# A transformer layer over 16 pairs of sequences: the loop over the middle pairs written out as straight code

## The chip, the cores and the metric

One Trainium2 chip, one of its cores. The metric is the device time of one execution in microseconds (us), as the median of several runs. The profile comes from one execution taken by the hardware profiler.

## The reference

The input `x` has 32 sequences of 256 tokens with 128 features. One layer of attention with eight heads and no scaling, then a feed-forward part, each followed by a residual sum and a layer norm without weights:

```python
Q = (x @ Wq.T).reshape(b, n, H, R)          # H = 8, R = 64
K = (x @ Wk.T).reshape(b, n, H, R)
V = (x @ Wv.T).reshape(b, n, H, d)          # d = 128
attn = softmax(einsum('bnhr,bmhr->bhnm', Q, K))
x = layernorm(x + einsum('bhnm,bmhd->bnd', attn, V))
h = silu(tlin(x, w1_w, w1_s)) * tlin(x, w2_w, w2_s)     # 512 wide
h = gelu(tlin(h, h1_w, h1_s)); h = gelu(tlin(h, h2_w, h2_s))
x = layernorm(x + tlin(h, w3_w, w3_s))
```

`tlin(x, w, s)` is `(x @ w.T) * s`. The matrices `w*_w` and `h*_w` hold whole numbers from a set of three.

## The kernel before

The 32 sequences are worked on as 16 pairs (`PAIRS = 16`) of 512 tokens. Every matrix product is made exact enough for float32 by splitting each operand into a high part and a low part in a narrower format (`t_hi` and `t_lo`, `pt_hi` and `pt_lo`, and so on) and adding two or three products (lines 778, 779 and 780 in `three`, lines 859 to 862 in `layer`). ScalarE (ACT) mostly makes the high parts, VectorE (DVE) and GpSimd (POOL) the low parts.

The work is a software pipeline written by hand. Step `i` has 16 slots, one for each of the 16 attention units of a pair (8 heads times 2 sequences). In a slot TensorE (PE) makes the scores of a unit three slots ahead, turns the probabilities of the present unit, and multiplies those of two slots ago by V. Beside this, step `i` carries the feed-forward part of pair `i - 1`: the turned x1 in slot 4, layer 1 in slots 5 to 8, layer 2 in slot 9 together with the V products of the next pair, layer 3 in slot 12 together with the T products of the next pair, layer 4 in slot 14 and, in slot 15, the turning back of its result (`turns(YT_BANK, ... yt ...)`, line 785, which the profile names `bank<-ident,turns_buf`). Step `i` also carries the last norm and the store of pair `i - 2`. There are thus 18 steps, 0 to 17, and the flags of a step (`cur`, `nxt`, `ffn`, `tail`) say which of these parts it has.

Each engine runs its own program: the helper `steps` is called once for each of SP, POOL, ACT, DVE and PE with that engine's `step`. The engines are held together by counting semaphores alone. Steps 0 and 1 are straight code. Steps 2 to 11 are a loop of five iterations with two steps in each, since some buffers alternate between even and odd pairs (`xt_of`). Steps 12 to 17 are straight code again. In the loop the number of the pair is a register: `count` builds the value that a semaphore must reach out of it, in straight code the value is a constant.

In every feed-forward layer PE looks at a flag that it has loaded from the weights, and takes one of two versions of the layer's code: with the products of the weights' low parts (`emit(True)`, line 862 runs too) or without them (`emit(False)`). This `either` is met seven times in a step: four times in layer 1, once in each of layers 2, 3 and 4.

Of the kernel before, what the change touches and what calls it, by code (L numbers as in the profile page):

```python
# [75 lines left out]
def layer_kernel(nc, x, wq, wk, wv, w1_w, w1_s, w2_w, w2_s, h1_w, h1_s, h2_w, h2_s, w3_w, w3_s, out):  # L76
# [3 lines left out]
    PAIRS = B // 2  # L80
# [18 lines left out]
    with ExitStack() as ctx:  # L99
# [113 lines left out]

        def steps(eng, step):

            step((None, 0), True, True, False, False)
            step((None, 1), True, True, True, False)

            last = (PAIRS - 3) // 2 * 2
            with eng.Fori(2, last - 1, 2) as r:  # L220
                step((r, 0), True, True, True, True)
                step((r, 1), True, True, True, True)
            for i in range(last, PAIRS + 2):
                step((None, i), i < PAIRS, i + 1 < PAIRS, i <= PAIRS, True)

        G_ATT = 4
        PREP = [(a_hi[:, 0:4, :], a_lo[:, 0:4, :]), (a_hi[:, 4:8, :], a_lo[:, 4:8, :]),
# [71 lines left out]
        def _(sp):  # L301
# [18 lines left out]
            def step(i, cur, nxt, ffn, tail):  # L320
# [6 lines left out]
                if exists(plus(i, 3)):  # L327
                    sp.wait_ge(s_xt_mm, count(i, 1, 3))
                    sp.dma_start(x_in[:, :, :], x_rows[row(plus(i, 3))]).then_inc(s_xin, 16)

            steps(sp, step)
            sp.wait_ge(s_yfree, 16 * PAIRS)

        @block.gpsimd
        def _(pool):
# [38 lines left out]
            def step(i, cur, nxt, ffn, tail):  # L374
                f, g = plus(i, -1), plus(i, -2)
                for j in range(J):
# [22 lines left out]
                    for c in range(KC):  # L399
                        if j == L2_SLOT and not tail:  # L400
                            lo_part(f, c, even_hi, even_lo, s_2hi, s_2lo)
                        if j == L3_SLOT and not alone(f):
                            lo_part(f, c, odd_hi, odd_lo, s_3hi, s_3lo)

            steps(pool, step)

        @block.scalar
        def _(act):
# [78 lines left out]
            def step(i, cur, nxt, ffn, tail):  # L487
                f, i1, i2 = plus(i, -1), plus(i, 1), plus(i, 2)
                for j in range(J):
# [56 lines left out]
                    if ffn and j == L4_SLOT:  # L546
                        act.wait_ge(s_l4, count(f, 1, 1))
                        if cur:
                            act.wait_ge(s_at, count(i, 2, 1))
                        nc.scalar.activation(yt[:, :], L4_BANK[:, :], ACT.Copy,  # L550
                                             scale=scales[:, 4 * KC:4 * KC + 1]).then_inc(s_yt, 1)

            steps(act, step)

        @block.vector
# [541 lines left out]
```

## Time and profile before

| | |
|---|---|
| median of 3 runs | 1096.17 us (1095.11 to 1096.27) |
| span of the profiled execution, first to last instruction | 1095.1 us |
| mean granted clock of TensorE over the span | 0.987 |
| PE busy | 1051.1 us, 96% |
| DVE busy | 819.5 us, 75% |
| ACT busy | 811.4 us, 74% |
| POOL busy | 602.9 us, 55% |

The time of the profiled execution outside its span is not recorded. The median lies 1.07 us above the span. In the views, a row with PE is a matmul, PEld its weight load, and a row with a q behind the engine's name is an instruction of that engine's sequencer, such as a branch or a sum in a register; these do not count as busy time.

### The profile page before, as it was taken

How to read it: one execution, taken by the hardware profiler on the slowest of the kernel's cores; microseconds unless marked ns; L12 is line 12 of the kernel's file. 1: busy time of each engine (PE TensorE's matmuls, PEld its weight loads, DVE VectorE, ACT ScalarE, POOL GpSimd, SP SyncE). 2: the span in 40 equal slices, each digit the busy share in tenths (PEclk: the TensorE clock that was granted, in tenths of full speed). 3: DMA queues.
4: the chain of work that ended last, by engine and by line, in shares of the span. 5: the costliest groups of instructions: out<-in, count | busy, mean ns of one | idle time of the engine just before them, and what ended most of it. 6: DMA issues, size and time to landing. Idle time of an engine off the chain costs nothing.

```text
span 1095.1 us, 20804 instructions
## 1 busy us (share of the span) xinstructions
PE 1051.1 (96%) x6598; PEld 932.7 (85%) x6598; DVE 819.5 (75%) x1722; ACT 811.4 (74%) x1948; POOL 602.9 (55%) x603
## 2 busy tenths in 40 slices
PE   7989999999999999999999998999999999999986
PEld 6878898888889879898798988889898888989864
DVE  5888687786868768687686966869687786968654
ACT  5768778787777867778687876878778787877732
POOL 1326457465565645557456564656657465655742
PEclk9999999999999999999999999999999999999987
DMA  6000000000000000000000000000000000000000
GB/s 173 11 10 12 1 21 2 20 12 21 13 11 21 1 22 12 10 21 2 22 12 11 21 11 13 11 20 12 11 21 1 20 12 11 11 11 11 9 3 20
DMA packets 29862, 18.31 MB, mean 17 GB/s; under 512 B 914, under 2 KB 28580, under 8 KB 29732
## 3 DMA queue, kind: packets, MB, share of 16 engines
q1 hardware_dynamic: 29732, 16.53, 5.2%
q8 instruction: 87, 1.43, 0.6%
q14 instruction: 43, 0.35, 0.1%
HBM read 12.33 MB, written 4.19 MB: 15 GB/s over the span
## 4 chain that ended last, share of the span: by engine, by line
PE 68%; DVE 11%; issue 10%; ACT 5%; POOL 5%; DMA 0%; SPq 0%; POOLq 0%; DVEq 0%; ACTq 0%
PE bank L859 13%; PE bank L860 12%; PE bank L778 11%; PE bank L780 11%; PE bank L779 11%; PE bank L785 8%; DVE neg_max L590 3%; ACT prob L441 2%; POOL prob L345 2%; DVE x L632 1%; DVE pt_lo L559 1%; POOL odd_lo L352 1%; POOL rstd L362 1%; ACT L441 1%; DVE t_lo L559 1%
## 5 line engine op out<-in xcount | busy, mean ns | idle before, releaser
L345 POOL TENSOR_TENSOR prob<-prob,inv_total 128x512 f32<-128x512 f32 x256 | 266.6, 1041 | 213.4 <-DVE inv_total L595 211.9
L441 ACT ACTIVATE prob<-bank,neg_max 128x256 f32<-128x256 f32 x512 | 237.7, 473 | 70.8 <-DVE neg_max L590 69.8
L352 POOL TENSOR_TENSOR odd_lo<-act,odd_hi 128x512 fp32r<-128x512 f32 x120 | 155.2, 1293 | 170.2 <-DVE odd_hi L657 117.0
L559 DVE TENSOR_TENSOR pt_lo<-bank,pt_hi 128x512 fp32r<-128x512 f32 x256 | 172.7, 675 | 60.6 <-ACT pt_hi L410 60.3
L590 DVE TENSOR_REDUCE neg_max<-bank 128x2 f32<-128x512 f32 x256 | 174.1, 680 | 11.5 <-PE bank L780 11.2
L410 ACT ACTIVATE pt_hi<-bank 128x512 fp32r<-128x512 f32 x256 | 149.6, 599 | 28.7 <-PE bank L785 26.8
L778 PE MATMUL bank<-pt_hi,v_hi 128*128 128x256 f32 x512 | 165.9, 324 | 0.0
L778 PE MATMUL bank<-xt_hi,t_hi 128*128 128x256 f32 x512 | 150.8, 295 | 14.9 <-issue 10.7
L785 PE MATMUL bank<-ident,prob 128*128 128x128 f32 x1024 | 155.2, 274 | 1.5 <-issue 0.7
L780 PE MATMUL bank<-xt_hi,t_lo 128*128 128x256 f32 x512 | 145.1, 283 | 0.0
L779 PE MATMUL bank<-xt_lo,t_hi 128*128 128x256 f32 x512 | 144.7, 283 | 0.0
L780 PE MATMUL bank<-pt_hi,v_lo 128*128 128x256 f32 x512 | 144.7, 283 | 0.0
L779 PE MATMUL bank<-pt_lo,v_hi 128*128 128x256 f32 x512 | 144.6, 282 | 0.0
L559 DVE TENSOR_TENSOR t_lo<-bank,t_hi 128x512 fp32r<-128x512 f32 x128 | 87.8, 688 | 46.4 <-ACT t_hi L410 45.4
L785 PEld LDWEIGHTS bank<-ident,prob 128*128 128x128 f32 x1024 | 118.3, 141 | 4.1 <-issue 2.9
L778 PEld LDWEIGHTS bank<-xt_hi,t_hi 128*128 128x128 f32 x512 | 97.2, 190 | 24.3 <-issue 16.7
L352 POOL TENSOR_TENSOR even_lo<-act,even_hi 128x512 fp32r<-128x512 f32 x60 | 77.4, 1290 | 67.8 <-DVE even_hi L657 65.3
L559 DVE TENSOR_TENSOR v_lo<-bank,v_hi 128x512 fp32r<-128x512 f32 x128 | 87.4, 686 | 31.9 <-ACT v_hi L410 30.5
L410 ACT ACTIVATE t_hi<-bank 128x512 fp32r<-128x512 f32 x128 | 76.7, 600 | 44.0 <-PE bank L780 42.6
L410 ACT ACTIVATE v_hi<-bank 128x512 fp32r<-128x512 f32 x128 | 76.9, 602 | 43.6 <-PE bank L780 43.0
L441 ACT ACTIVATION_READ_ACCUMULATOR prob<-bank,neg_max 128x1 f32 x512 | 104.1, 203 | 0.0
L779 PEld LDWEIGHTS bank<-xt_lo,t_hi 128*128 128x128 f32 x512 | 97.6, 191 | 4.7
(116 smaller groups left out, 2555.7 us busy)
## 6 DMA issues: line engine op xcount, KB each, us to landing
x_in<-in_L_attn_x SPq DMA_DIRECT2D x16, 256.0 KB, 2.8
res<-in_L_attn_x SPq DMA_DIRECT2D x16, 256.0 KB, 2.7
out_x<-y SPq DMA_DIRECT2D x16, 256.0 KB, 2.3
h_in<-in_L_ffn_h_w SPq DMA_DIRECT2D x2, 1024.0 KB
w_in<-in_L_ffn_w_w SPq DMA_DIRECT2D x3, 256.0 KB
wv_in<-in_L_attn_Wv SPq DMA_DIRECT2D x1, 512.0 KB, 5.9
wq_in<-in_L_attn_Wq SPq DMA_DIRECT2D x1, 256.0 KB, 4.1
wk_in<-in_L_attn_Wk SPq DMA_DIRECT2D x1, 256.0 KB, 5.0
```

The source lines that it names most:

```text
L345: nc.gpsimd.tensor_tensor(prob[:, j % RING, :, :], prob[:, j % RING, :, :], inv_total[:, j % RING, :].unsqueeze(2).to_broadcast([P, NT, N] ...
L352: nc.gpsimd.tensor_tensor(lo[:, c, :], act_of(f, c), hi[:, c, :].bitcast(F32), ALU.subtract).then_inc(s_lo, 1)
L410: return nc.scalar.activation(dst, src, ACT.Copy)
L441: last = nc.scalar.activation(prob[:, j % RING, nt, :], sc[j % 2][:, nt * N:(nt + 1) * N], ACT.Exp, bias=neg_max[:, j % RING, nt:nt + 1], ...
L559: return nc.vector.tensor_tensor(dst, src, hi.bitcast(F32), ALU.subtract)
L590: nc.vector.tensor_reduce(neg_max[:, j % RING, :], sc[j % 2].rearrange("p (t m) -> p t m", m=N), AX.X, ALU.max, negate=True).then_inc(s_ma ...
L778: mm(dst, w_hi, m_hi, start=start, stop=False)
L779: mm(dst, w_hi, m_lo, start=False, stop=False)
L780: return mm(dst, w_lo, m_hi, start=False, stop=stop)
L785: last = turn(dst[:, n * P:(n + 1) * P], b, ident[:, :])
L859: mm(dst, w_hi[c], m_hi[c], start=(c == 0), stop=False)
L860: last = mm(dst, w_hi[c], m_lo[c], start=False, stop=(c == n - 1 and not with_lo))
```

## The change

The loop and the special cases before it are replaced by one Python loop over all 18 steps, which runs when the program is built. The code of each step stands in the program once, ten steps of it where there were two. The flags of every step are the same as before: `1 <= i <= PAIRS` is false for step 0 and true for step 1, `i >= 2` is false for both, and the other expressions give what the calls had written out. Each value that a semaphore is compared with is now a constant in every step, and each address of a pair in DRAM too. Nothing else is changed: no engine gets, loses or reorders an instruction of arithmetic, a transfer or a wait.

```diff
         def steps(eng, step):
 
-            step((None, 0), True, True, False, False)
-            step((None, 1), True, True, True, False)
-
-            last = (PAIRS - 3) // 2 * 2
-            with eng.Fori(2, last - 1, 2) as r:
-                step((r, 0), True, True, True, True)
-                step((r, 1), True, True, True, True)
-            for i in range(last, PAIRS + 2):
-                step((None, i), i < PAIRS, i + 1 < PAIRS, i <= PAIRS, True)
-
-
+            for i in range(PAIRS + 2):
+                step((None, i), i < PAIRS, i + 1 < PAIRS, 1 <= i <= PAIRS, i >= 2)
```

## Rows read from the trace of the kernel before

**Rows 1.** The page: busy time by engine, and the granted clock in 40 slices.

```profile
PE 1051.1 (96%) x6598; PEld 932.7 (85%) x6598; DVE 819.5 (75%) x1722; ACT 811.4 (74%) x1948; POOL 602.9 (55%) x603
PEclk9999999999999999999999999999999999999987
```

**Rows 2.** The page: the chain of work that ended last, by engine.

```profile
PE 68%; DVE 11%; issue 10%; ACT 5%; POOL 5%; DMA 0%; SPq 0%; POOLq 0%; DVEq 0%; ACTq 0%
```

**Rows 3.** Waits of PE, whole span: us in total, times, longest.

```profile
PE bank L778 <- issue: 10.7, 4, 2.9
...
PE bank L785 <- DVE x L632: 4.6, 8, 3.2
```

**Rows 4.** Timeline of PE: start, duration, the instruction, idle time before it.

```profile
277.81 0.38 PE L778 MATMUL bank<-xt_hi,t_hi 128*128 128x256 f32 x1 [2.46 <-issue]
...
410.14 0.38 PE L778 MATMUL bank<-xt_hi,t_hi 128*128 128x256 f32 x1 [2.58 <-issue]
...
542.52 0.38 PE L778 MATMUL bank<-xt_hi,t_hi 128*128 128x256 f32 x1 [2.70 <-issue]
...
673.67 0.38 PE L778 MATMUL bank<-xt_hi,t_hi 128*128 128x256 f32 x1 [2.95 <-issue]
```

**Rows 5.** Line 220, the loop: times, duration in ns (min/median/max), first and last start.

```profile
L220 PEldq COMPARE_BRANCH  x5: 76/3517/3880, 274.2 to 802.2; - x5
...
L220 DVEq COMPARE_BRANCH  x5: 50/56/67, 275.5 to 803.5; - x5
...
L220 ACTq COMPARE_BRANCH  x5: 40/45/45, 275.6 to 803.6; - x5
```

**Rows 6.** Stretches: length, busy us (instructions) of each engine, granted clock, DMA.

```profile
277.81:281.69 3.88, 3.88 (x20) 3.88 (x21) 2.51 (x5) 1.51 (x5) 1.06 (x1) 0.56 0.03 6
...
542.52:546.10 3.58, 3.58 (x30) 3.58 (x31) 2.56 (x6) 1.68 (x6) 1.06 (x1) 1.00 0.03 7
...
802.75:806.00 3.25, 3.25 (x30) 3.25 (x29) 2.94 (x8) 2.27 (x9) 2.25 (x4) 1.00 0.00 0
```

**Rows 7.** Timeline of PE: the turning back in slot 15, once a step.

```profile
146.09 0.60 PE L785 MATMUL bank<-ident,turns_buf 128*128 128x128 f32 x4
210.32 0.60 PE L785 MATMUL bank<-ident,turns_buf 128*128 128x128 f32 x4
274.75 0.60 PE L785 MATMUL bank<-ident,turns_buf 128*128 128x128 f32 x4
342.53 0.60 PE L785 MATMUL bank<-ident,turns_buf 128*128 128x128 f32 x4
406.95 0.60 PE L785 MATMUL bank<-ident,turns_buf 128*128 128x128 f32 x4
...
539.22 0.60 PE L785 MATMUL bank<-ident,turns_buf 128*128 128x128 f32 x4
605.70 0.60 PE L785 MATMUL bank<-ident,turns_buf 128*128 128x128 f32 x4
670.12 0.60 PE L785 MATMUL bank<-ident,turns_buf 128*128 128x128 f32 x4
...
802.75 0.60 PE L785 MATMUL bank<-ident,turns_buf 128*128 128x128 f32 x4
867.23 0.60 PE L785 MATMUL bank<-ident,turns_buf 128*128 128x128 f32 x4
931.52 0.60 PE L785 MATMUL bank<-ident,turns_buf 128*128 128x128 f32 x4
```

**Rows 8.** Line 73, where wait values are counted: sequencer instructions, times, duration in ns.

```profile
L73 PEldq ALU_OP  x175: 32/32/36, 145.8 to 797.9; - x175
L73 ACTq ALU_OP  x20: 35/35/38, 147.9 to 680.4; - x20
```

**Rows 9.** Line 867, the branches of the feed-forward layers: times, duration in ns.

```profile
L867 PEldq COMPARE_BRANCH  x112: 200/217/359, 93.0 to 1076.4; - x112
```

**Rows 10.** The page: DMA queues of instructions, packets, MB, share of 16 engines.

```profile
q8 instruction: 87, 1.43, 0.6%
```

## The prediction

> **What bounds the kernel now.** I read the page first. PE is busy for 96% of the span, no other engine for more than 75% [rows 1], and the chain that ended last runs over PE for 68% [rows 2]. So the time is set by how fast PE gets through its list, and a pause of PE is lost unless something else had been about to hold it anyway. The clock line shows full speed nearly everywhere, up to the last two slices [rows 1].
>
> The second view is the list of PE's waits. Its largest entry is not a wait for an engine: "issue" means that PE had nothing to run and that no semaphore held it, so its sequencer had not delivered. It happened 4 times for 10.7 us in total [rows 3]. The timeline places the four gaps before the same matmul, the first of slot 0, at 277.81, 410.14, 542.52 and 673.67 [rows 4], about 132 us apart. A loop of five iterations takes its branch back four times, and falls through at the fifth.
>
> The third view is the loop's own line. PE's sequencer took 76 ns for the quickest of its five branches, 3517 for the median one and 3880 for the longest, the first of them from 274.2 on [rows 5]. With the median of 3.5 us it ends at 277.7, just before the matmul at 277.81. DVE's and ACT's branches on the same line took at most 67 ns [rows 5]. So the pause is one of PE's sequencer at the jump back to the loop's head. The reader is to see three views agree on it: the count, the place, the duration.
>
> The fourth view tells what follows a gap. In the 3.88 us after the first one the granted clock averages 0.56, and 20 matmuls run; after the exit from the loop, with no gap, 30 run in 3.25 us at clock 1.00 [rows 6]. In that stretch the clock was at its lower level, 1.2 GHz, for most of the time, after PE had stood still for 2.46 us. After the third gap it stayed at 2.4 GHz [rows 6].
>
> **What a step costs.** The turning back in slot 15 happens once a step, so its starts measure the steps [rows 7]:
>
> - straight code, from step 12 to 13: 931.52 - 867.23 = 64.29 us, and from step 1 to 2, where only the first end is straight: 210.32 - 146.09 = 64.23;
> - the loop without the branch: 406.95 - 342.53 = 64.42, 670.12 - 605.70 = 64.42, and 274.75 - 210.32 = 64.43;
> - the loop with the branch: 342.53 - 274.75 = 67.78, and after the third gap, the one without a slow clock, 605.70 - 539.22 = 66.48.
>
> **The change part by part.**
>
> 1. The branch back on PE goes, four times. Over a plain loop step it costs 67.78 - 64.43 = 3.35 us at the first and 66.48 - 64.42 = 2.06 at the third. At the third the gap was 2.70 [rows 4], so about 0.65 of it was no loss: while PE stood, the other engines caught up, and PE later met shorter waits, such as the one for x1 in slot 4, which stands in the list with 4.6 us in 8 times [rows 3]. At the first, gap 2.46 minus 0.65 leaves 1.8, and the other 1.5 is the slow clock. The four together: the two-step iterations are 406.95 - 274.75 = 132.20, 539.22 - 406.95 = 132.27, 670.12 - 539.22 = 130.90 and 802.75 - 670.12 = 132.63. Four times two loop steps of 64.42 are 515.36, and the sum is 528.00. Some 12.6 us go with the branch.
>
> 2. The sums in registers go. In the loop PE's sequencer makes 175 of 32 ns for wait values alone, ACT's 20 of 35 [rows 8]. They do not fill PE's matmul list by themselves, since the sequencer runs ahead of the matmuls, but all of them lie before a wait or after a release on some engine. What they cost is the difference between a loop step and a straight one: 64.42 - 64.29 = 0.13 us in each of ten steps, 1.3 or 1.4 us. This is the soft term. It rests on one clean straight interval; the interval from step 11 to 12, the first outside the loop, is 867.23 - 802.75 = 64.48 and shows no gain. I take 64.29, since that straight interval has no loop code at either end. Its lower bound is nothing.
>
> 3. Work that is added: the instructions of eight more steps have to be fetched once each rather than again and again. The number executed does not grow. The fetch queue of whole blocks moved 1.43 MB in 87 packets for 0.6% of the DMA engines' time [rows 10], beside matmuls that read nothing from DRAM. In the straight steps 12 to 13 the fetches go on and PE loses nothing. Price zero; it is covered by the matmuls already queued in PE, and if that cover failed it would show as the same kind of gap, 2.46 us or more.
>
> 4. ACT's, DVE's, POOL's and SP's loop branches go too. They cost at most 67 ns on DVE and 45 on ACT [rows 5], lie off PE's path, and are part of term 2 where they count at all.
>
> The sum in one figure, without the parts: from 210.32 to 867.23 are ten steps, 656.91 us [rows 7]. Ten straight steps are 642.9. The difference is **14.0 us**. The steps outside are not touched. The profiled span of 1095.1 becomes 1081.1. The median of the runs lies 1.07 above the span, which I take over: 1096.17 - 14.0 = **1082.2 us**.
>
> One rule agrees with these rows and speaks on both sides of the change. The Trainium skill, page "Runtime: NRT & Kernel Launch", section "Instruction fetch mechanics", says that a sequencer fetches its code ahead only in order, in blocks of 16 KiB, and that a branch taken to a target outside the blocks at hand stalls until that block has come. The 3517 ns of the branch back fit that. The branches of `either` are jumps too, and by the same rule the straight code could stall at them, at new places relative to the blocks; that is the second rival below.
>
> **The rivals.**
>
> *The gap does not belong to the branch.* Something due every second step could starve PE at that place; then only the branch instruction goes, at 76 ns [rows 5] five times, 0.4 us: 1095.8, no change. Against it: the fifth branch, which falls through, takes 76 ns and has no gap behind it, though the step is otherwise the same, and no gap stands at the ends of steps 1, 12 and 13. The Trainium skill, page "Advanced Engine Details and Errata", section "Control Flow Timing", gives a compare-and-branch some 108 ns; by it alone the change would bring an estimated 0.5 us. The median of 3517 ns goes against it here. Chance 3%.
>
> *Slower: forward jumps that stall.* Each new straight step has seven branches of line 867 on PE, 70 in the ten steps, and each jumps over a version of a layer's code. If one lands in code that is not there, it costs what a loop branch does, 2.1 to 3.8 us. The change is a loss once more than 14.0 / 3.35 = 4.2 of the 70 do so, that is five or more; with one in every step, at 3.35, the time would be 1082.2 + 33.5 = 1115.7. What speaks for it: these are the same kind of jump. Against it: 112 of them ran, 14 places in the loop and 42 outside, and the longest took 359 ns [rows 9], and PE's four long gaps are all at line 220. 56 places without one stall make five in 70 unlikely. Chance 3% for slower, 5% for one to three stalls with a gain left, 1085.6 to 1092.3.
>
> *Only the branch term comes.* The ten steps stay at 64.42 rather than 64.29: 1096.17 - 12.6 = 1083.6. This is the low end of the main case. Chance 20%.
>
> *The pauses helped.* ACT, DVE and POOL catch up in each gap, 0.65 us worth. Without gaps they could fall behind and hold PE. The steps after the loop speak against it: 64.48 and 64.29, not rising [rows 7]. A fall-behind of 0.1 us a step would make the time 1083.2. It lies in the same range.
>
> **How the numbers follow.** The sum as it stands, 1082.2, has 69%, the branch term alone 20%; together 89%, with a range of their own from 1081.0 (steps at 64.23, which saves 14.6, and 0.6 for half the spread of the three runs) to 1084.2. A few stalls 5%, slower 3%, no change 3%. The range given, 1080.5 to 1086.0, adds one stalled jump at 3.8 above and some room for the runs' spread below. A measurement of this kernel can tell about 0.2%, 2.2 us, from no change. Faster by more than that: 0.94; within: 0.03; slower: 0.03.
>
> **What the profile after would show.** The entry "issue" before line 778 is gone from PE's waits, and no branch of line 220 exists. The slot-15 turnings are 64.3 us apart from step 2 to step 13, odd and even alike. The granted clock's mean rises from 0.987 to about 0.992: a slow stretch took 0.44 of 3.88 us [rows 6], 1.7, and three of them are 0.5% of the span; the rest of the loss, at the end, stays. PE's busy time falls by about 3 us (14.0 less the 10.7 of idle time), and the span by 14. The sums in registers of line 73 are gone. Instruction packets of the block queue stay near 85. The prediction would be wrong if new "issue" gaps of 2 to 3 us stood behind branches of line 867 or at the blocks' ends, or if the plain steps took 64.4 and more with waits of PE for another engine.

## The result, and the profile after

The changed kernel took 1083.55 us (median of 4 runs, 1082.70 to 1084.39), the kernel before 1096.20 (4 runs, 1095.11 to 1096.27). The ratio is 0.9884, with a 95% interval of 0.9872 to 0.9896. The profiled execution had a span of 1080.6 us, 14.5 less than before, and took 1082.89 in all.

The first lines of the page, to be read against [rows 1], [rows 2] and [rows 10]:

```profile
span 1080.6 us, 19355 instructions
PE 1045.8 (97%) x6598; PEld 927.6 (86%) x6598; DVE 818.3 (76%) x1722; ACT 816.2 (76%) x1948; POOL 603.4 (56%) x603
...
PEclk9999999999999999999999999999999999999988
...
q8 instruction: 76, 1.25, 0.5%
...
PE 67%; DVE 15%; issue 7%; ACT 6%; POOL 5%; DMA 0%; SPq 0%; ACTq 0%; POOLq 0%; DVEq 0%
```

The number of matmuls is the same. PE is busy for 5.3 us less, above all the time that its matmuls had lost at the lower clock, and the other 9.2 us of the span were idle time of PE. The mean granted clock rose from 0.987 to 0.993 (predicted 0.992). The block queue moved 76 packets, 11 fewer; the prediction had them stay near 85.

The list of PE's waits, against [rows 3]:

```profile
PE bank L776 <- DMA x_in<-in_L_attn_x: 4.2, 1, 4.2
PE bank L769 <- ACT prob L432: 3.9, 6, 1.5
PE bank L776 <- DVE x L623: 3.2, 1, 3.2
```

Lines are 9 lower than before, so line 769 is the former 778. The entry "issue" of 10.7 us before it is gone. The one for x1 (line 623, formerly 632) fell from 4.6 us in 8 times to 3.2 in one; that one comes near the end of the span and stood in the kernel before too, and the small ones of the middle steps are gone.

The turning back in slot 15, against [rows 7]:

```profile
210.06 0.60 PE L776 MATMUL bank<-ident,turns_buf 128*128 128x128 f32 x4
...
274.37 0.60 PE L776 MATMUL bank<-ident,turns_buf 128*128 128x128 f32 x4
...
338.63 0.60 PE L776 MATMUL bank<-ident,turns_buf 128*128 128x128 f32 x4
...
853.01 0.60 PE L776 MATMUL bank<-ident,turns_buf 128*128 128x128 f32 x4
917.34 0.60 PE L776 MATMUL bank<-ident,turns_buf 128*128 128x128 f32 x4
```

The step that held the first branch back now takes 338.63 - 274.37 = 64.26 us, where it took 67.78. Ten steps take 853.01 - 210.06 = 642.95; the prediction said 642.9. The eleven marks of steps 2 to 12, taken one by one, are 64.26 to 64.34 us apart. And the stretch behind the mark at 274.37, where before a gap of 2.46 and then a slow clock stood [rows 4, 6]:

```profile
274.37:277.62 3.25, 3.25 (x31) 3.25 (x30) 2.94 (x8) 2.37 (x9) 2.31 (x4) 1.00 0.02 5
```

PE is busy for all of it, at clock 1.00. The branches of the feed-forward layers, the place of the slower rival, took no more than in [rows 9]:

```profile
L858 PEldq COMPARE_BRANCH  x112: 200/210/340, 92.7 to 1062.7; - x112
```

### The profile page after: what moved, and what is told of

It reads as the page before. It is cut to its first block, busy times and chain, and to the rows that moved or that the text cites. A ratio compares the mean times of both kernels' runs of the same rounds, so it can differ in the third digit from the quotient of the medians.

```text
span 1080.6 us, 19355 instructions
## 1 busy us (share of the span) xinstructions
PE 1045.8 (97%) x6598; PEld 927.6 (86%) x6598; DVE 818.3 (76%) x1722; ACT 816.2 (76%) x1948; POOL 603.4 (56%) x603
## 4 chain that ended last, share of the span: by engine, by line
PE 67%; DVE 15%; issue 7%; ACT 6%; POOL 5%; DMA 0%; SPq 0%; ACTq 0%; POOLq 0%; DVEq 0%
PE bank L850 13%; PE bank L851 13%; PE bank L769 11%; PE bank L771 11%; PE bank L770 11%; PE bank L776 7%; DVE neg_max L581 4%; DVE x L623 4%; POOL prob L336 3%; DVE pt_lo L550 3%; ACT prob L432 2%; ACT L432 2%; POOL rstd L353 1%; ACT pt_hi L401 1%; DVE t_lo L550 1%
## 5 line engine op out<-in xcount | busy, mean ns | idle before, releaser
L459 ACT ACTIVATE act<-bank,scales 128x512 f32<-128x512 f32 x120 | 82.6, 690 | 25.1 <-PE bank L851 22.7
```

## The experiments

Each was timed beside runs of the kernel before on the same chip. "Ten steps" is always the time from the slot-15 mark of step 2 to that of step 12.

**PE alone straight, and PE alone in the loop.** `steps` got a flag, set for PE only, and in the second kernel for all but PE:

```diff
-        def steps(eng, step):
+        def steps(eng, step, straight):
+            if straight:
+                for i in range(PAIRS + 2):
+                    step((None, i), i < PAIRS, i + 1 < PAIRS, 1 <= i <= PAIRS, i >= 2)
+                return
...
-            steps(pe, step)
+            steps(pe, step, True)        # False in the second kernel, the other four reversed
```

> PE alone gets the straight code, the other four engines keep the loop. Theory: the loss is PE's stall at its own branch back. The four gaps and the three slow-clock stretches go, which is 12.6 us of the ten steps (656.9 to 644.3); of the 1.4 us of register sums only PE's part goes, so ten steps take 642.9 to 644.3 and the median is 1082 to 1085. Rival, the pause belongs to the loop of the other engines (PE waits for something that they deliver late): nothing or little goes, 1094 to 1096.

> The reverse: PE alone keeps the loop, the others are straight. Theory: the four gaps of 2.5 to 3.0 us before the first matmul of slot 0 stay, and only what the register sums of the others cost goes, 0 to 1.4 us: ten steps 655.5 to 656.9, median 1094.8 to 1096.2. Rival: the median falls to about 1083.

With PE alone straight: 1084.02 us (1082.69 to 1084.70) against 1095.60, ratio 0.9898 (0.9881 to 0.9914); ten steps 853.57 - 209.19 = 644.38, 0.1 above the upper end of what was expected. With PE alone in the loop: 1094.19 (1090.96 to 1096.83), ratio 0.9988 (0.9974 to 1.0003); ten steps 863.88 - 210.34 = 653.54. In that one PE's waits read (the one-sided kernels have four lines more, so line 782 is the former 778)

```profile
PE bank L782 <- issue: 9.8, 4, 2.7
```

and its branches of the loop's line

```profile
L224 PEldq COMPARE_BRANCH  x5: 76/3297/3634, 274.1 to 799.0; - x5
```

The four gaps follow PE's loop and nothing else. So do the 11 packets of the block queue: it moved 87 with PE alone in the loop and 76 with PE alone straight. All four kernels execute ten such steps, so these are packets that PE's branches back added, some three to a branch taken.

The loops of the others are not quite free, though. In the ten steps of the kernel with PE alone straight, PE waited four times for ACT, which it never did there in the changed kernel:

```profile
PE bank L782 <- ACT prob L445: 3.4, 4, 1.0
```

The marks of the profile with PE alone in the loop show two things more:

```profile
342.24 0.60 PE L789 MATMUL bank<-ident,turns_buf 128*128 128x128 f32 x4
...
406.58 0.60 PE L789 MATMUL bank<-ident,turns_buf 128*128 128x128 f32 x4
...
472.61 0.60 PE L789 MATMUL bank<-ident,turns_buf 128*128 128x128 f32 x4
```

A plain loop step of PE, with the other engines free of register sums, is 406.58 - 342.24 = 64.34 us, where straight steps took 64.30 in the mean and 64.26 to 64.34 one by one: PE's own 530 register instructions cost some 0.04 us a step, which is not clear of that spread. And the next step, with a gap, is 66.03, while two others in this run took 67.6 and 67.9. Ten steps came out 2 us below the expected range (and the median 0.6 below) because the clock fell behind two of the four gaps rather than three:

```profile
277.63:281.10 3.47, 3.47 (x18) 3.47 (x19) 2.23 (x5) 1.38 (x5) 1.06 (x1) 0.58 0.02 5
409.54:413.00 3.46, 3.46 (x29) 3.46 (x30) 2.45 (x5) 1.65 (x6) 1.06 (x1) 1.00 0.02 5
```

Both stretches follow a gap of 2.36 us; behind the first the clock fell, behind the second it did not.

**The loop form without a branch taken back.** Each pair of steps in a loop of its own that runs once:

```diff
-            with eng.Fori(2, last - 1, 2) as r:
-                step((r, 0), True, True, True, True)
-                step((r, 1), True, True, True, True)
+            for k in range(2, last, 2):
+                with eng.Fori(k, k + 2, 2) as r:
+                    step((r, 0), True, True, True, True)
+                    step((r, 1), True, True, True, True)
```

> Each pair of steps stands in the program once, but each in a loop of its own that runs once: the values waited for are still made from a register, and each such loop ends in a branch that is not taken back. Theory: no gap, no slow clock; what stays is the register term, 0.13 us a step: ten steps 644.2 against 642.95 of the changed kernel, span 1081.9 against 1080.6, median 1084.9 against 1083.55. Rival, the 0.13 us a step was not the register sums but something of the taken branch: ten steps 642.9 to 643.1. Rival, the branch instruction itself costs: gaps again, five of them.

1083.01 us (1082.74 to 1083.36), ratio 0.9887 (0.9871 to 0.9904). The marks and the branches:

```profile
210.25 0.60 PE L786 MATMUL bank<-ident,turns_buf 128*128 128x128 f32 x4
...
854.02 0.60 PE L786 MATMUL bank<-ident,turns_buf 128*128 128x128 f32 x4
```

```profile
L221 PEldq COMPARE_BRANCH  x5: 76/76/80, 274.0 to 789.1; - x5
```

Ten steps take 643.77, so the register sums are worth 643.77 - 642.95 = 0.8 us, not 1.4, and the branches taken back 656.91 - 643.77 = 13.1. The ten steps lie between the 644.2 that was expected and the 642.9 to 643.1 of the first rival. They rest on one profile of this kernel; three profiles without loops, two of them further down, gave 642.95 to 643.07. The median is 1.9 below the expected 1084.9 and does not differ from that of the changed kernel. A branch that falls through takes 76 to 80 ns and leaves no gap.

**The branch announced.** The loop stays, with a hint at the head of each iteration that names the branch back. It is meant to have the code at the branch's target fetched ahead:

```diff
-            with eng.Fori(2, last - 1, 2) as r:
+            with nc.Fori(2, last - 1, 2, engines=bass.OrderedEngineSet([eng.engine]),
+                         hint_back_edge=True) as r:
```

> The kernel before with its loop, but every engine's branch back is announced at the head of each iteration, so that the block with the loop's head can be fetched ahead of the branch. Theory, the stall is the fetch of that block: PE's branches take well under 1 us, the gaps and the slow clock go, and the register sums stay: ten steps about 644.3 plus 4 times at most 0.3, median 1083.6 to 1085.5. Rival, the stall is the taken branch's own work (emptying the queue, starting anew): PE's branches still take 3.4 us and the median stays at 1096.

1088.09 us (1086.14 to 1089.79), ratio 0.9938 (0.9921 to 0.9955), 2.6 above the expected range.

```profile
L220 PEldq BRANCH_PREFETCH_HINT  x5: 45/45/45, 144.2 to 659.6; - x5
...
L220 PEldq COMPARE_BRANCH  x5: 85/339/343, 272.9 to 788.0; - x5
```

The same taken branch took 339 ns instead of 3517, and none of the four gaps nor a slow clock was left in the loop. So the stall is the fetch of the code at the target. But a new loss came where the fifth branch falls through. The step behind the loop takes 856.43 - 788.64 = 67.79:

```profile
788.64 0.60 PE L785 MATMUL bank<-ident,turns_buf 128*128 128x128 f32 x4
...
856.43 0.60 PE L785 MATMUL bank<-ident,turns_buf 128*128 128x128 f32 x4
```

VectorE's timeline shows one cause, some 9 us behind the fifth branch, between two instructions of the same kind, with nothing to wait for in the second:

```profile
797.06 0.18 DVE L613 BATCH_NORM_AGGREGATE mv<-stats 128x2 f32<-128x6 f32 x1
799.87 0.18 DVE L613 BATCH_NORM_AGGREGATE mv<-stats 128x2 f32<-128x6 f32 x1 [2.62 <-issue]
```

The theory was that the last hint had sent DVE for the loop's head, so that the code that came next was late. But the same trace shows two gaps of PE in this step, and only the second is a wait for DVE:

```profile
795.80 0.33 PE L785 MATMUL bank<-ident,turns_buf 128*128 128x128 f32 x1 [1.36 <-issue]
...
800.77 0.63 PE L785 MATMUL bank<-ident,prob 128*128 128x128 f32 x4 [1.32 <-DVE pt_lo L559]
```

To see whether it was DVE's hint alone:

```diff
-                         hint_back_edge=True) as r:
+                         hint_back_edge=eng.engine == nc.tensor.engine) as r:
```

> The loop stays on all engines, and only PE's branch back is announced at the head of the iteration. With the hint on all engines the four gaps went, but after the fall-through VectorE stood 2.6 us without an instruction and the step behind the loop took 67.8 us. Theory: that loss came from DVE's own hint, which made it fetch the loop's head in place of the code that follows the loop. Without it no step takes over 64.6 us, ten steps 643.8 to 645, median 1083.5 to 1085.5. Rival: PE's hint alone does the same to PE's own code, one gap of 2.5 to 3.5 us behind the fifth branch, ten steps 647 to 648, median 1087 to 1088.5.

1085.48 us (1084.47 to 1088.35), ratio 0.9917 (0.9891 to 0.9944), ten steps 857.20 - 210.95 = 646.25. DVE's gap of 2.6 us went with DVE's hint, and the step behind the loop shortened from 67.79 to 857.20 - 790.86 = 66.34. But the theory that it was DVE's hint alone fell, since PE's hint does the same to PE:

```profile
796.39 0.27 PE L785 MATMUL bank<-ident,turns_buf 128*128 128x128 f32 x1
799.05 0.33 PE L785 MATMUL bank<-ident,turns_buf 128*128 128x128 f32 x1 [2.39 <-issue]
```

The gap stands between two matmuls of one and the same `turns`. The rival had it right in kind; its lower ends were too high by 0.1 us for the gap, 0.75 for the ten steps and 1.5 for the median, which lies within the theory's range. That the engine had fetched the loop's head instead fits this and is not shown. A second finding is in the waits of ACT and PE in the steps of the loop:

```profile
ACT pt_hi L410 <- issue: 7.0, 4, 1.8
```

```profile
PE bank L778 <- ACT prob L441: 7.2, 10, 1.5
```

Now that PE no longer stalls, ACT's own branch back leaves ACT without an instruction for 1.8 us four times, and PE waits for it: 7.2 us in 10 times against 3.9 in 6 in the changed kernel, so 0.8 a time. In the profile with the hint on all engines ACT has no such entry, and PE waits for `prob` 3.9 us in 6 times, so the gap belongs to ACT's branch. That the branch itself took at most 45 ns [rows 5] did not show it. In the kernel before, ACT has no "issue" entry either; its stall most likely lay under PE's own there.

**Fewer branches.** Two iterations of four steps, so that one branch is taken back:

```diff
-            last = (PAIRS - 3) // 2 * 2
-            with eng.Fori(2, last - 1, 2) as r:
-                step((r, 0), True, True, True, True)
-                step((r, 1), True, True, True, True)
+            last = 10
+            with eng.Fori(2, last - 1, 4) as r:
+                for n in range(4):
+                    step((r, n), True, True, True, True)
```

> The kernel before with four steps to an iteration: two iterations (steps 2 to 9), one branch taken back instead of four, eight steps with register sums instead of ten. Theory: one gap of 2.5 to 3 us before the first matmul of slot 0, one step of 66.0 to 68.2 us, the others 64.3 to 64.43; ten steps 644.7 to 648, median 1084.9 to 1088. Rival, the loss belongs to the loop as such and not to each branch: ten steps above 652.

1088.90 us (1088.08 to 1089.52), ratio 0.9937 (0.9918 to 0.9955); ten steps 859.82 - 211.28 = 648.54.

PE's entry "issue" and its branches:

```profile
PE bank L778 <- issue: 2.4, 1, 2.4
```

```profile
L220 PEldq COMPARE_BRANCH  x2: 76/1689/3302, 404.6 to 666.2; - x2
```

One gap for one branch, and a step of 472.79 - 405.20 = 67.59 with it, as expected. The median is 0.9 us above the range and the ten steps 0.5; the rival, above 652, is out. Four of the other steps took 64.75 to 64.78, some 0.35 more than a plain loop step, with short waits of PE for x1 and for `pt_lo` of DVE. DVE has two gaps of 0.4 "issue" in two of them. What makes these is open.

**Longer forward jumps.** The slower rival was a stall at the branches of the feed-forward layers. To find from where on it would be real, the version of layer 4 that is jumped over was written several times, in the changed kernel; 24 in place of 12 in the second:

```diff
-                layer(L4_BANK[:, :], ..., with_lo, s_3lo, count(f, KC, 1)).then_inc(s_l4, 1)
+                for n in range(12 if with_lo else 1):
+                    last = layer(L4_BANK[:, :], ..., with_lo, s_3lo, count(f, KC, 1))
+                last.then_inc(s_l4, 1)
```

> The changed kernel, in which the version of layer 4 that is not taken is written 12 times over: the branch of layer 4, once a step in steps 1 to 15, jumps over some 290 instructions rather than 24. The version is never run here, so nothing is computed otherwise. Theory, a forward jump stalls only when it leaves the block at hand and the one fetched ahead: 0 to 4 stalls of 3 us in 15, median 1083 to 1096. The Trainium skill, page Runtime: NRT & Kernel Launch, section Instruction fetch mechanics, gives a block 256 instructions; by it such a jump ends in the next block mostly, and one further on at times. Rival, forward jumps never stall: 1083.5. Rival, every one out of its block does: 15 stalls, about 1130.

> The same with 24 copies: each of the 15 jumps passes some 580 instructions. Theory: the target is never there, 15 branches of the feed-forward layers take over 3 us, PE shows 15 gaps, and the time rises by 15 times 2.1 to 3.8: 1115 to 1140. Rival, forward jumps do not stall or PE keeps far more code: 1083.5.

The jumps were 16, not 15; step 16 has a layer 4 too. With 12 copies: 1089.71 us (1087.95 to 1090.72), ratio 0.9944 (0.9927 to 0.9962). With 24: 1101.01 (1096.46 to 1104.97), ratio 1.0042 (1.0023 to 1.0060), slower than the kernel before. The changed kernel beside them had 1082.98. Branches and waits with 12 copies:

```profile
L858 PEldq COMPARE_BRANCH  x112: 200/210/3764, 93.1 to 1070.1; - x112
```

```profile
PE bank L850 <- issue: 10.1, 8, 1.7
```

and with 24:

```profile
L858 PEldq COMPARE_BRANCH  x112: 200/215/5022, 92.9 to 1085.4; - x112
```

```profile
PE bank L850 <- issue: 24.6, 15, 3.0
```

Taken one by one, 9 of the 16 branches of layer 4 took 2.1 to 3.8 us with 12 copies and the other 7 took 0.4 or less; with 24 copies all 16 took 3.3 to 5.0. So about half of the jumps of some 290 instructions miss their code, and all of those of some 580. The theory had 0 to 4 stalls in the first case, so its picture of one block at hand and one fetched ahead is too kind, or incomplete; why the nine come in three runs of three steps, with three quick ones between, is open. The mechanism of the slower rival is real, and the changed kernel is clear of it because its jumps are short. The price was sized too high: 18.0 us for 16 jumps is 1.1 each, not 2.1 to 3.8, and the median of 1101.01 lies far below the 1115 to 1140 expected. PE has more matmuls queued when it comes to this branch. One with 24 copies, and the matmuls around its end:

```profile
L858 PEldq COMPARE_BRANCH  x1: 3329/3329/3329, 603.3 to 603.3; - x1
```

```profile
604.90 0.60 PE L776 MATMUL bank<-ident,x_in 128*128 128x128 f32 x4
606.79 0.47 PE L850 MATMUL bank<-odd_hi,w_hi 128*128 128x512 f32 x1 [1.29 <-issue]
```

PE had work until 605.50, for 2.2 us of the branch. At the loop's first branch, at 274.2, it had work until 277.81 - 2.46 = 275.35 [rows 4, 5], for 1.15 us. Another of the gaps with 24 copies, the longest:

```profile
209.21 0.60 PE L776 MATMUL bank<-ident,x_in 128*128 128x128 f32 x4
212.78 0.63 PE L850 MATMUL bank<-odd_hi,w_hi 128*128 128x512 f32 x1 [2.97 <-issue]
```

The stretches behind the two gaps:

```profile
212.78:216.30 3.52, 3.52 (x9) 2.74 (x10) 0.69 (x4) 0.00 (x0) 0.00 (x0) 0.52 0.02 5
...
606.79:610.00 3.21, 3.21 (x19) 2.85 (x20) 1.83 (x7) 1.64 (x5) 0.60 (x1) 1.00 0.25 75
```

After the idle time of 2.97 us the clock fell to the level of 1.2 GHz, after 1.29 it did not.

**No forward branches at all.** In the changed kernel only the version without the weights' low parts is written:

```diff
-                with pe.If(any_lo[0]):
-                    emit(True)
-                with pe.Else():
-                    emit(False)
+                emit(False)
```

> The changed kernel with the branches of the feed-forward layers taken out of PE's code: only the version without the low parts of the weights is written, so weights with low parts would be computed wrongly; these have none. PE has no branch but the last one, 112 fewer at about 0.21 us each of sequencer time, and its code is shorter by the versions not taken. Theory, a branch whose target is at hand is hidden behind the matmuls already queued: ten steps 642.5 to 643, median within 1 us of the changed kernel's 1083. Rival, each costs PE its 0.2 us: 7 a step, 14 us over the ten, median 1069 or less.

1082.03 us (1081.60 to 1082.37), ratio 0.9875 (0.9857 to 0.9893); ten steps 853.20 - 210.17 = 643.03, the same as with the branches. So the 112 branches, of 200 to 340 ns each in the changed kernel, are hidden behind PE's queued matmuls. The median lies 1 us below the 1083.0 that the changed kernel had beside the jumps; by the ratios to the kernel before, 0.9875 and 0.9888 with intervals that overlap, that is no difference shown.

**The changed kernel once more**, beside the jumps:

> The changed kernel once more, beside the others of this call. Ten steps 642.95 us again, no gap of PE between 150 and 980 us; median 1082.7 to 1084.4 as in the first four runs, and the time outside the span about 1.8 us as in the runs of the kernel before that stood beside the first four experiments.

1082.98 us (1082.67 to 1083.45) against 1096.22, ratio 0.9888 (0.9859 to 0.9918); ten steps 853.16 - 210.09 = 643.07. The time outside the span was 1.8 to 2.3 us.

## Why the prediction was right

**The branch back on PE** was the cause, as its first term said. That it belongs to PE's own loop is shown by the two one-sided kernels, that it needs the branch to be taken by the loops that run once, and that it is the fetch of the target by the hint, which brought the same branch from 3517 to 339 ns. The term was 12.6 us by the prediction and measured 13.1. Both figures start from the same profile of before, in which the clock fell behind three of four gaps; with two falls, as in the profile of PE alone in the loop, the term would have been some 1.3 to 1.9 us smaller. One reading was loose: the first branch back took 3392 ns, not the median's 3517, and ended at 277.6. The first rival, a gap that does not belong to the branch, is out.

**The branches of the other engines** were put off PE's path, by the 45 and 67 ns that they take. That holds in the kernel before, where PE stalls longer. With PE straight and the others in the loop, PE waited for ACT four times, 3.4 us in all, and the ten steps took 644.38, 0.6 more than with no branch taken back on any engine (643.77), although PE had no register sums left. The change takes these branches away as well, so the sum did not suffer from it.

**The register sums** were sized at 1.4 us and measured 0.8. The 0.5 or 0.6 between the two terms had been drawn from the wrong side: 64.42 for a loop step was taken as free of the branch, but part of its distance to 64.29 goes away with the branches as well, since loop steps without a taken branch take 643.77 / 10 = 64.38. How much of it is PE's own is not settled: plain steps with PE alone in the loop took about 64.33, which puts some 0.4 of the 0.8 on PE, with single straight steps 0.08 apart. The sum of the two terms, 13.96 us over ten steps, is what was predicted, 14.0.

**The fetch of the added code** costs nothing, as said: 642.95 for ten steps against ten times 64.29. That the two agree to 0.05 us is in part luck, since 64.29 was one step and such steps turned out at 64.26 to 64.34.

**The forward jumps** do not stall, as forecast. The reason was argued from 56 places without a stall; the runs with longer jumps show that it no longer holds at some 290 instructions. Its price in the rival, 2.1 to 3.8 against 1.1 measured, was too high by a factor of 2 to 3.4. It was taken from the loop's branch, before which PE has less queued.

**The pauses helped** did not come about: steps 3 to 12 take 64.26 to 64.34 with no rise.

**Only the branch term comes** named 1083.6, and the median is 1083.55. By the median alone this rival, with its 20%, did better than the sum. The ten steps decide against it: they take 642.95 where it had 644.2.

**PE's busy time** fell by 5.3 us and not by about 3. The prediction took the whole 10.7 us of gaps as idle time saved, though by its own first term 0.65 of each gap had been no loss, since PE later met shorter waits. By its own figures that is 10.7 - 2.6 = 8.1 of idle time and 5.9 of busy time, against 9.2 and 5.3 measured.

**The packets of the block queue** were to stay near 85 and came to 76. That executed code is fetched the same number of times was right, but the branches back had cost 11 packets on top.

**The measured 1083.55 is 1.35 above 1082.2**, inside the range. The span came out at 1080.6, 0.5 below the 1081.1 predicted: the stretches before and after the ten steps were 0.26 and some 0.2 us shorter. The miss is in the last step, span to median. It used a median less the span of another execution, 1.07 us. In the later runs of the kernel before, each with its own span, the difference is 1.8 (1.76 to 1.94). So the profiled span of before, 1095.1, lay some 0.7 above what belongs to its median, and the median gains less than 14.0 by that much. The other half of the miss is in the first runs of the changed kernel, which spent 1.9 to 2.8 us outside their spans. The two whose mean is the median, 1082.89 and 1084.21, had spans of 1080.6 and 1081.4, in the mean 1081.0 as predicted, and 2.3 and 2.8 us outside. What made that part longer was not found. In the second comparison the gain is 13.2.

## What to carry to other kernels

A loop with a long body can pay for a fetch of its head at each branch taken back: here 2.5 to 3 us of idle time on PE, and 1.8 on ACT. How short a body must be to escape it was not tried. Look for "issue" before the same instruction once an iteration, and at the duration of the branch itself, before touching the loop; a short branch alone does not clear an engine, as ACT showed. Writing the code out removed it for all engines, and announcing the branch removed most of it but brought a new gap behind the fall-through. If the straight code contains jumps over versions not taken, keep the skipped code short: at some 290 instructions nine of sixteen stalled, and with 580 the whole gain was lost.

## What was not expected of the hardware

The clock does not fall behind every gap. In the profiles here it fell behind gaps of 2.46, 2.58 and 2.95 us in the kernel before and not behind one of 2.70; with PE alone in the loop behind 2.36 and 2.70 and not behind another 2.36; with 24 copies behind 2.97 and not behind 1.29. So the length of the gap alone does not decide it. A step with a slow clock is some 1.3 to 1.9 us longer than one with a gap alone, and the number of such falls changes from run to run. This fits the spread of the kernel before, 1092.02 to 1097.80 us over its later runs, where all eight runs of the changed kernel lie within 1082.67 and 1084.39. That the falls make the whole spread is inferred from the mean clocks of the runs (0.992 for the one with the shortest span, 1090.2, and 0.987 to 0.990 for those of 1094.5 and more), not from a profile of each.
